# Constant matmuls inside a quantised attention

## The reference, cut to what matters

```python
wq = quant_weight(qkv_w, qkv_alpha, 4)
qkv = einsum('bnc,oc->bno', x, wq).reshape(B, N, 3, 16, 4).transpose(2, 0, 3, 1, 4)
q = quant_act(qkv[0] + bias_q, q_alpha, q_zp, 4) * SCALE      # codes -8..7
k = quant_act(qkv[1] + bias_k, k_alpha, k_zp, 4)
v = quant_act(qkv[2], v_alpha, v_zp, 4)
attn = softmax(einsum('bhnd,bhmd->bhnm', q, k), axis=-1)
attn = quant_act(attn, attn_alpha, attn_zp, 8)               # 8 bits
out = einsum('bhnm,bhmd->bhnd', attn, v)
```

## Time and profile before

| | us |
|---|---|
| median of three runs | 843.94 |
| lowest, highest | 838.22, 846.42 |
| the profiled execution | 842.1 |
| its span, first to last instruction | 839.5 |
| PE busy | 670.8 (80%) |
| DVE busy | 616.5 (73%) |
| ACT busy | 520.1 (62%) |
| POOL busy | 169.6 (20%) |
| mean granted clock of PE | 0.826 |

### The profile page before, as it was taken

The page is one execution under the profiler, slowest core; times in us unless marked ns, Lnnn a source line. Parts: engine busy times, 40 slices in busy tenths (PEclk is TensorE's granted clock), DMA queues, the critical chain, the costliest instruction groups (busy, mean ns, idle before and its releaser), DMA issues.

```text
span 839.5 us, 12933 instructions
## 1 busy us (share of the span) xinstructions
PE 670.8 (80%) x4514; PEld 400.6 (48%) x4514; DVE 616.5 (73%) x1349; ACT 520.1 (62%) x1237; POOL 169.6 (20%) x169
## 2 busy tenths in 40 slices
PE   7589976777889889679987878577888695779866
PEld 3222231543556556445555545254656543446545
DVE  7882348468999897777777765999676669986864
ACT  4479977654778778145775764645665475565742
POOL 5030040012889789711000000000000000000000
PEclk8879987887555555956999998879999897899998
DMA  9400000000000000000000000000000000000000
GB/s 300 140 1 1 2 2 0 1 0 1 1 2 1 1 2 1 1 0 1 2 1 1 2 2 0 1 0 1 2 2 1 1 0 1 0 2 1 1 1 25
DMA packets 9059, 10.54 MB, mean 13 GB/s; under 512 B 2746, under 2 KB 7844, under 8 KB 8868
## 3 DMA queue, kind: packets, MB, share of 16 engines
q1 hardware_dynamic: 8996, 9.73, 3.6%
HBM read 9.21 MB, written 0.52 MB: 12 GB/s over the span
## 4 chain that ended last, share of the span: by engine, by line
PE 43%; DVE 36%; ACT 11%; issue 9%; POOL 1%; DMA 0%; ACTq 0%; DVEq 0%; POOLq 0%
PE ps L1390 4%; PE ps L1650 4%; PE ps L1553 4%; DVE s_nmB L1032 3%; DVE s_nmD L1311 3%; PE ps L1633 3%; ACT arena L514 2%; PE ps L1737 2%; PE ps L1540 2%; PE ps L1670 2%; PE ps L1461 2%; PE ps L1745 2%; PE ps L1831 2%; PE ps L1433 2%; PE ps L1812 2%
## 5 line engine op out<-in xcount | busy, mean ns | idle before, releaser
L382 POOL TENSOR_SCALAR arena<-arena,s_rB,s_zpu 128x512 uint8<-128x512 f32 x128 | 115.9, 945 | 42.5 <-DVE s_rB L1005 41.2
L552 ACT ACTIVATE arena<-ps,s_nmB 128x512 f32<-128x512 f32 x128 | 86.6, 683 | 31.8 <-DVE s_nmB L1032 31.2
L574 ACT ACTIVATE arena<-ps,s_nmx 128x512 f32<-128x512 f32 (+3 forms) x128 | 60.7, 527 | 50.2 <-DVE s_nmx L1130 49.7
L1032 DVE TENSOR_REDUCE s_nmB<-ps 128x2 f32<-128x1024 f32 x64 | 77.3, 1217 | 6.9 <-PE ps L1540 6.6
L1125 DVE TENSOR_REDUCE s_nmx<-ps 128x1 f32<-128x512 f32 (+3 forms) x128 | 56.6, 484 | 21.4 <-PE ps L1636 20.9
L514 ACT ACTIVATE arena<-ps 128x1024 f32<-128x1024 f32 x64 | 60.9, 1026 | 6.4 <-PE ps L1445 6.4
L1553 PE MATMUL ps<-cst,arena 128*128 128x128 f32 x256 | 61.0, 417 | 1.7 <-POOL arena L382 0.8
L1396 PE MATMUL ps<-ones 128*128 128x512 f16 x134 | 43.9, 491 | 22.7 <-ACT s_wn L485 6.6
L1540 PE MATMUL ps<-staged 8*128 8x512 f16 x128 | 46.7, 585 | 11.7 <-ACT arena L552 10.9
L1553 PEld LDWEIGHTS ps<-cst,arena 128*128 128x128 f32 x256 | 48.7, 218 | 14.7 <-POOL arena L382 8.2
L1650 PE MATMUL ps<-cst,arena 128*128 128x128 f32 x320 | 46.9, 301 | 8.7 <-issue 5.3
(11 more groups left out here) (344 smaller groups left out, 1515.3 us busy)
## 6 DMA issues: line engine op xcount, KB each, us to landing
vec<-in_vec SPq DMA_DIRECT2D x1, 1882.0 KB, 11.7
w_d<-in_wqkv SPq DMA_DIRECT2D x2, 768.0 KB
vec<-in_vec SPq DMA_DIRECT2D x1, 960.0 KB, 8.2
w_h<-in_w SPq DMA_DIRECT2D x2, 341.0 KB
x_tok<-in_x SPq DMA_DIRECT2D x1, 512.0 KB, 4.1
arena<-in_w_f SPq DMA_DIRECT2D x2, 256.0 KB, 8.0
rope<-in_rope SPq DMA_DIRECT2D x1, 512.0 KB, 10.5
w_do<-in_wo SPq DMA_DIRECT2D x2, 256.0 KB
```

The lines of the kernel that those rows point to most:

```text
L382: nc.gpsimd.tensor_scalar(u8[:, n % 4, j // 2, :, 2 * (j % 2)], prob[:, n % 2, j * 512:j * 512 + 512], sm("rB", 8)[:, c:c + 1], sm("zpu", ...
L552: nc.scalar.activation(prob[:, n % 2, j * 512:j * 512 + 512], ps[:, j, :], ACT.Exp, bias=sm("nmB", 8)[:, c:c + 1], accum_out=sm("sumB", 8) ...
L574: nc.scalar.activation(probC[:, n % 2, at(qt):at(qt) + w], ps[:, bank, col:col + w], ACT.Exp, bias=nmx[:, TB * b + qt, h:h + 1]).then_inc( ...
L1032: free(V.tensor_reduce(sm("nmB", 8)[:, c:c + 2], ps[:, 2 * half:2 * half + 2, :], X, ALU.max, negate=True), "maxB")
```

## The change

`keep_busy` takes a bank. In B's loop on PE, between the first score pair and the transposes of codes, steps 3, 4, 7, 8, 11, 12, ... 28, 31 get constant matmuls into bank 7: 12 in step 3, 4 in each of the 14 others. Ahead of them PE waits for `stagedB`, DVE's copy of the turned operands that bank 7 last held: for the second copy in steps 3 and 4, the third in 7 and 8, and so on up to the eighth.

```diff
-            def keep_busy(n):
+            def keep_busy(n, bank=5):
 
                 for _ in range(n):
-                    M(ps[:, 5, :], ones16[:, :], ones16[:, 0:1].to_broadcast([P, 512]), start=True, stop=True)
+                    M(ps[:, bank, :], ones16[:, :], ones16[:, 0:1].to_broadcast([P, 512]), start=True, stop=True)
...
             for n in range(B * H + 4):
                 if n < B * H:
                     s_b(n, (0, 1))
+                    if n >= 3 and n % 4 in (0, 3):
+                        pe.wait_ge(sem["stagedB"], min((n + 1) // 4 + 1, 4 * B))
+                        keep_busy(4 if n > 3 else 12, 7)
                 if 3 <= n < B * H + 3:
                     pt_b(n - 3)
                 if n < B * H:
```

## The result

The changed kernel takes 860.06 us in the median (859.14 to 862.46, 4 runs) against 845.18 us before: a ratio of 1.0186, 95% interval 1.015 to 1.0222, 14.9 us slower. The profiled execution has a span of 858.6 us.

The account below looks back on a forecast made before the run. POOL's 3.78 us a step was taken to bound the attention stage, PE at half clock close beside it. Terms 4.5 + 9.6 + 1.5 + 3.0 - 1.5 = +17.1 on 842.1 gave 859.2, stated as 858 us; range 843 to 867.

Parts of the forecast that it names:

- step 3: Step with twelve constants: second score pair and reduce late, unhidden because DVE's scaling of the second batch follows; +4.5 us.
- steps 7 to 27 with n%4 = 3: Six steps whose constants wait for bank 7's copy and run at half clock, 1.6 us each; +9.6 us.
- step 31: Step with four constants and no newer copy of bank 7 to wait for; +1.5 us.
- steps with n%4 = 0: Five uncovered steps, 12 to 28, each 1.5 us late at half clock, put at 4 in 10; +3.0 us.
- given back: Gain from full clock in steps 1 and 2 of each group, as far as POOL's pace allows; -1.5 us.
- loop: Sixteen-head quantised attention, from first score pair to start of POOL's last step; the forecast's terms sum to +17.1 us.
- POOL's pace as the bound, PE beside it: In the attention stage POOL's 3.78 us a step sets the pace; PE at half clock takes 3.74.
- ceiling of 9.6: DVE's waits for PE in the whole stage, 6.6 and 3.0 us: the most any faster PE can give.
- Slices: Profile page's time slices: in 10 to 17, the attention stage, TensorE's clock was said to stand at 5, half speed.
- The new wait: Constants write bank 7, so PE first waits for DVE's copy of it, not yet done in steps with n%4 = 3.
- The rival "never back": Clock rises once at step 3, falls, and four constants don't regain it; +27.5 less 1, 868 us; chance 0.13.
- The 0.04 us of slack: What PE at half clock has in hand each step: 3.74 us against POOL's 3.78.

Follow-up runs that it names:

- bank 4: The changed kernel's 68 constants at the same places but into bank 4, without the wait for bank 7's copy, against the kernel before: 856.06 us, ratio 1.0127.
- the kernel with the groups alone: The changed kernel's 14 places of 4 constants without the 12 of step 3, against the kernel before: 855.35 us, ratio 1.0148.
- the late kernel: The same 68 constants and wait, placed behind the second score pair instead of ahead of the transposes, against the kernel before: 848.85 us, ratio 1.0047.

## Why the prediction was right, point by point

The forecast was 858 us, slower, by the delay of each step's second score pair; measured 860.06. Its terms, read from POOL's starts in both profiles (step 3 counted from the first score pair):

| term | forecast | measured |
|---|---|---|
| step 3 | 4.5 | 3.2 |
| steps 7 to 27 with n%4 = 3 | 9.6 | 11.0 (1.20, 1.93, 1.84, 1.80, 2.22, 1.98) |
| step 31 | 1.5 | 1.1 |
| steps with n%4 = 0 | 3.0 | 1.1 (step 24 alone) |
| given back | -1.5 | -0.9 |
| loop | 17.1 | 15.5 |

- *The number.* 858 against 860.06 is nearer than the sum earned, and in part luck. The loop grew 1.6 us less than the 17.1, and inside it an underestimate (steps 7 to 27, by 1.4) stood against two overestimates (step 3 by 1.3, n%4 = 0 by 1.9). Outside the loop, where I had put nothing, the two profiles differ by 3.6 us in code that is the same.
- *POOL's pace as the bound, PE beside it.* Right for the quiet steps: POOL's 3.78 us stands at full clock too, and a PE that is lighter by 0.3 us a step gained 1.6 us, well under the ceiling of 9.6. But 0.26 of the 3.78 is the hand-over, not POOL's work, and a period under 3.78, which I had called a sign that POOL isn't the bound, stood in the profile before already (3.49 at step 2). What came back in the changed kernel is 0.9 where I had 1.5: 0.6 at step 20 and little at steps 9, 10, 14 and 18, less 0.4 lost at step 26.
- *Slices.* In the earlier trace rows the clock is 5 in six slices, 210 to 336 us. Of the slices 10 to 17 that I named, the first stands at 7 and the last at 9; the loop only touches them. No term hangs on this.
- *The new wait.* Right in kind: alone +4.0, and taking it away saves 4.3. At step 23 it was longer than at any other (3.10 us ahead of the constants), since DVE's output of the first batch precedes the copy; I had not seen this.
- *Half clock at n%4 = 3.* Right in six of six places. The price was 1.8 us on average, not 1.6: at step 11 the reduce came 2.1 us late and POOL 1.9, so 0.2 us was in hand where I took off 0.7. The clock over the loop was 0.66; I had expected 0.7 to 0.8.
- *n%4 = 0.* The size was off: I put half clock at 4 in 10, and it was so at step 24 of the five that aren't covered. The long wait of step 11 and its kind may be the reason: it puts more time between the places, so that full clock has come by the next one. Without the wait (bank 4) three of the five ran at half clock and cost. That is argued from one profile of each; no experiment shows it.
- *Step 3.* The size was off: the pair was 3.8 late, not 4.5, since full clock came within the twelve (4.67 us), and DVE's scaling, now without POOL beside it, took 1.91 instead of 2.54 us and gave 0.6 back.
- *Where DVE waits.* I named its copy of codes and its second reduce as waiting, but looked for the idle time ahead of the reduce. It is ahead of the copy of codes, which comes first in DVE's order and needs the transposes that the constants delay.
- *The rule on transposes.* The Trainium skill (TensorE: Matmul & The Clock Gate, Part 4: PE-mode transpose) says that full clock doesn't engage for transposes, which don't count as busy in the same way. The trace disagrees for these transposes: 32 of them alone were followed by full clock in the earlier trace rows. The rival "never back" didn't happen either: the kernel with the groups alone had 0.66 over the loop. There transposes follow every four constants, so no run here shows what the four do by themselves.
- *What I said besides the sum.* That 1.7 us on PE would cost the same wherever they stand, stated ahead of the late kernel, was wrong. The 0.04 us of slack is a mean over a group in quiet steps. In the steps with DVE's extra work PE has a gap behind the second pair, while ahead of it DVE waits for what the constants hold back.

## What to carry to other kernels

A low clock on an engine is no bottleneck until a lighter version of that engine's work has been seen to gain; here 10 us less work on PE were worth 1.6. Constant matmuls run at the low clock exactly where they are meant to end it, so they must stand where their engine waits for others in any case, behind the instruction that the next engine needs, and in a bank whose reader is done. The same 68 matmuls cost 15.5 us of the loop ahead of the second score pair and 3.3 behind it. With a choice of 36 in gaps the loop was 0.5 us shorter and the kernel 0.5% faster, which the loop explains only in small part. And two small instructions can set the pace between two large engines: look at what ends last before each step.

## What the runs showed of the hardware

Constants in every step didn't hold the clock: the mean granted clock over the loop was 0.82 with 4 to each step and 0.75 with 2.

The granted clock also moves the time of code that nobody changed. From POOL's last step to the first score of the next attention it took 29.0 us before, at a mean clock of 0.79, and 33.0 in the kernel with only the wait, at 0.66, with the same instructions there. The windows (the first is before's), and the projection inside each:

```profile
333.80:362.80 29.00, 17.46 (x129) 12.64 (x129) 20.66 (x44) 6.91 (x12) 17.09 (x17) 0.79 0.00 1
```
```profile
336.80:369.80 33.00, 22.08 (x128) 16.14 (x128) 21.20 (x44) 7.12 (x12) 17.07 (x17) 0.66 0.00 1
```
```profile
346.85 5.43 PE L1390 MATMUL ps<-arena,uT 128*128 128x384 f32 x16 [0.22 <-ACT uT L456]
```
```profile
352.21 7.16 PE L1390 MATMUL ps<-arena,uT 128*128 128x384 f32 x16
```

Over the eleven profiles whose instructions there are the same it lay between 28.5 and 33.4 us. That is as large as most effects measured here, so a single profile tells of the loop, and only the medians of many runs tell of the kernel.

DVE's work on the second batch ran faster without POOL beside it. In step 3 its two instructions took 1.04 and 1.50 us in the kernel with late constants (shown above), while POOL was busy, and 0.95 and 0.96 us in the changed kernel, where POOL was idle for 5.32 us.
